# Spreading the shared expert of a mixture-of-experts layer over seven routed experts

## The chip, the cores and the metric

The kernel runs on one core of one Trainium2 chip. The metric is the device time of the whole launch in microseconds. The kernel before took 1259.23 us (median of three runs, 1257.9 to 1260.51). The profile shows one execution of its own, which took 1258.86 us and whose traced span is 1257.0 us.

Engine names in the rows: PE is the matrix engine (TensorE), PEld its weight loads, DVE the vector engine, ACT the scalar engine, POOL GpSimd, SP the sync engine, which here does nothing but wait on semaphores and issue DMAs.

## The reference, cut to what matters

A Perceiver layer on 256 tokens of width 512: cross-attention to 25088 context rows, self-attention with 16 heads, and a mixture of experts. The change is in the last part alone:

```python
shared_out = silu(x @ shared_gate_w) * (x @ shared_up_w) @ shared_down_w    # 512 -> 1024 -> 512
logits = x @ gate_w
topk_ids = argmax(logits); topk_val = max(logits)                           # one of 32 experts for a token
xs = x * sigmoid(topk_val)[:, None]
g = ragged_dot(sorted xs, routed_gate_w)                                    # 32 x 512 x 1024
u = ragged_dot(sorted xs, routed_up_w)                                      # 32 x 512 x 1024
d = ragged_dot(silu(g) * u, routed_down_w)                                  # 32 x 1024 x 512
out = x + shared_out + routed_out                                           # all in float32
```

Every expert has three matrices of 2 MB (2048 KB) each, a gate, an up and a down part. The 32 routed experts are 96 such loads, and all of them are read whatever the routing is.

## The kernel before, in words

The cross-attention fills the span up to about 635 us, then come its last projections, the self-attention (to about 765 us), the router, and from 784.97 us on the experts.

Each engine runs a program of its own, written in the order in which it runs; semaphores tie them together. Nothing is scheduled: what stands later in an engine's program starts later.

**Places for weights.** SBUF holds three sets of places, numbered 0 to 2, each with a place for a gate (`wg`), an up (`wu`) and a down matrix (`wd`), 2 MB each, and one more place for a single gate matrix, `wg_early`, which lies where the token tables of later experts go. Place 0 first holds the shared expert; places 1 and 2 first hold experts 0 and 1; `wg_early` holds the gate of expert 2. These ten loads are issued before the first expert runs (L344 to L366). Every later load goes into a place that some expert has finished with, so SP waits for `gate_done`, `up_done` or `down_done` of that expert, or for `sh_gate_in_psum`, `sh_up_in_psum` or `sh_down_done` of the shared one (L382 to L409). SP's program is one line: a load whose place is free still stands behind an earlier load that waits. All loads go through one queue.

**A routed expert** (`expert`, L794) has up to 32 tokens (a slot tile). PE multiplies gate (L802) and up (L808), ACT makes silu (L1022), DVE the product `hh` (L1347), PE transposes it (L821), ACT copies it out as `hh_t` (L1026), PE multiplies down (L832), DVE copies the result out as `dd` (L1358), and PE scatters it to the tokens into PSUM banks 4 and 5 (L842).

**The shared expert** works on all 256 tokens and is cut into 16 chunks of its gate (0 to 7) and up part (8 to 15), `shared_chunk` (L752), and 8 pieces of its down part (L857). Chunks 0 and 1 run before expert 0. Experts 0 to 3 take three chunks each, put where PE would otherwise wait: behind the up matmuls, behind the transposes, and behind the down matmuls. Then follow, with no routed expert between them, chunks 14 and 15, the eight pieces of the down part in one run, and the token tables of experts 8 to 31.

**Token tables.** `tokens_to_slots` (L778) multiplies the tokens with a selection matrix for eight experts at a time and ACT copies the result out (`slots_out`, L1009). Part 0 is made ahead of expert 0, parts 1 to 3 in one run ahead of expert 4.

**The ring.** From expert 4 on, expert e uses place (e - 4) mod 3, and SP loads expert e + 3 as expert e finishes each of its matrices.

The end: the last expert has matmuls on an identity matrix (`keep_warm`, L462) in its waits, then DVE adds the result to `x` (L1398), which SP stores (L424).

Of the kernel before, what the change touches and what calls it, by code (L numbers as in the profile page):

```python
# [30 lines left out]
E = 32  # L31
FI = 1024
IC = FI // P
GE = 8
SLOT = 32
OV = NQ // SLOT - 1
RING = 3
JG = P // SLOT
# [6 lines left out]
assert NB * BLK == NK and NB % 2 == 1 and (E - 2) % RING == 0 and NSEL == HC * P  # L45
# [21 lines left out]
def perceiver_layer(nc, a):  # L67
    with ExitStack() as ctx:
# [156 lines left out]
        gw_loaded0 gw_loaded1 gw_loaded2 uw_loaded0 uw_loaded1 uw_loaded2 dw_loaded0 dw_loaded1 dw_loaded2  # L225
# [46 lines left out]
        places = [1, 2, 0]  # L272
# [24 lines left out]
        def _(sp):  # L297
# [68 lines left out]
            sp.dma_start(flat(wg_early), g2).then_inc(gw_loaded[1], 16)  # L366
# [12 lines left out]
            g4, u4, d4 = expert_weights(4)  # L379
            g5, u5, d5 = expert_weights(5)  # L380
            g6, u6, d6 = expert_weights(6)
# [3 lines left out]
            sp.wait_ge(s["up_done"], 1)  # L385
            sp.dma_start(flat(wu[1]), u2).then_inc(uw_loaded[1], 16)
            sp.wait_ge(s["down_done"], 1)
            sp.dma_start(down_flat(wd[1]), d2).then_inc(dw_loaded[1], 16)
            next_expert(3, 2, done=2)
            sp.wait_ge(s["sh_gate_in_psum"], IC)  # L390
            sp.dma_start(flat(wg[0]), g4).then_inc(gw_loaded[0], 16)
            sp.wait_ge(s["up_done"], 3)
            sp.dma_start(flat(wu[1]), u5).then_inc(uw_loaded[1], 16)
            sp.wait_ge(s["down_done"], 3)
            sp.dma_start(down_flat(wd[1]), d5).then_inc(dw_loaded[1], 16)
            sp.wait_ge(s["gate_done"], 4)
            sp.dma_start(flat(wg[2]), g6).then_inc(gw_loaded[2], 16)
            sp.wait_ge(s["sh_up_in_psum"], IC)
            sp.dma_start(flat(wu[0]), u4).then_inc(uw_loaded[0], 16)
            sp.wait_ge(s["up_done"], 4)  # L400
            sp.dma_start(flat(wu[2]), u6).then_inc(uw_loaded[2], 16)
            sp.wait_ge(s["sh_down_done"], 1)
            sp.dma_start(down_flat(wd[0]), d4).then_inc(dw_loaded[0], 16)
            sp.wait_ge(s["down_done"], 4)
            sp.dma_start(down_flat(wd[2]), d6).then_inc(dw_loaded[2], 16)
            next_expert(7, 0, done=5)
            with sp.Fori(2, (E - 2) // RING) as g:
                for k in range(RING):
                    next_expert(g * RING + 2 + k, places[k], done=g * RING + k)  # L409
# [46 lines left out]
        def _(pe):  # L456
# [337 lines left out]
            def expert(n, k, rnd, first=False, last_one=False, gate_w=None, shared=()):  # L794

                gate_w = wg[k] if gate_w is None else gate_w
                pe.wait_ge(s["xg_ready"], n + 1)
                pe.wait_ge(gw_loaded[k], rnd)
# [18 lines left out]
                if shared:  # L817
                    shared_chunk(shared[0])
# [4 lines left out]
                if shared:  # L823
                    shared_chunk(shared[1])
# [10 lines left out]
                if shared:  # L835
                    shared_chunk(shared[2])
# [8 lines left out]

            expert(0, 1, 16, first=True, shared=(2, 3, 4))
            expert(1, 2, 16, shared=(5, 6, 7))
            expert(2, 1, 32, gate_w=wg_early, shared=(8, 9, 10))
            expert(3, 2, 32, shared=(11, 12, 13))
            shared_chunk(14)  # L850
            shared_chunk(15)
            pe.wait_ge(s["sh_h_ready"], IC)

            pe.wait_ge(dw_loaded[0], 16)
            for i in range(IC):
                for t in range(QT):
                    last = mm(ps[:, 4 + t, :], h_t[:, i, t * P:(t + 1) * P], wd[0][:, i, :], start=False, stop=True,  # L857
                              skip_group_check=True)
            last.then_inc(s["sh_down_done"], 1)

            for part in range(1, E // GE):
                tokens_to_slots(part)
            expert(4, 0, 32)
            with pe.Fori(1, (E - 2) // RING - 1) as g:
                for k in range(RING):
                    expert(g * RING + 2 + k, places[k], g * 16 + 32)
            for k in range(RING):
                expert(E - RING + k, places[k], 16 * ((E - 2) // RING + 1), last_one=(k == RING - 1))
            pe.wait_ge(s["overflow_known"], 1)
            more = pe.value_load(eo_i[0:1, 7:8], min_val=0, max_val=OV)  # L870
            with pe.If(more > 0):
                tokens_to_slots(E // GE)
                with pe.Fori(0, OV) as o:
                    expert(o + E, 0, o * 16 + 16 * ((E - 2) // RING + 2))
# [3 lines left out]
        def _(act):  # L878
# [141 lines left out]
            def expert(n, more=True, shared=()):  # L1020
                act.wait_ge(s["gate_done"], n + 1)
                act.activation(sg[:, :], ps[:, 0, 0:GW], ACT.Silu).then_inc(s["silu_ready"], 1)  # L1022
                if shared:
                    shared_silu(shared[0])
# [5 lines left out]
                for i in shared[1:]:  # L1030
                    shared_silu(i)
# [5 lines left out]
            expert(0, shared=(2, 3, 4))  # L1037
            expert(1, shared=(5, 6, 7))
            expert(2)
            expert(3)  # L1040
            for part in range(1, E // GE):
                slots_out(part)
            expert(4)
            with act.Fori(1, (E - 2) // RING - 1) as g:
                for k in range(RING):
                    expert(g * RING + 2 + k)
# [13 lines left out]
        def _(dve):  # L1060
# [283 lines left out]
            def expert(n, first=False, shared=()):  # L1344
# [10 lines left out]
                for i in shared[:2]:  # L1355
                    shared_h(i)
                dve.wait_ge(s["down_done"], n + 1)
                dve.tensor_copy(dd[:, :], ps[:, 3, :]).then_inc(s["d_ready"], 1)  # L1358
                for i in shared[2:]:
                    shared_h(i)  # L1360

            expert(0, first=True)
            expert(1)
            for part in range(1, E // GE):
                selection(part)
            expert(2, shared=(0, 1, 2))
            expert(3, shared=(3, 4, 5))
            shared_h(6)
            shared_h(7)
# [17 lines left out]
            expert(4)  # L1387
            with dve.Fori(1, (E - 2) // RING) as g:
                for k in range(RING):
                    expert(g * RING + 2 + k)  # L1390
# [44 lines left out]
```

## Time and profile before

| what | value |
|---|---|
| median of three runs | 1259.23 us |
| the profiled execution | 1258.86 us |
| its span | 1257.0 us |
| first routed expert starts | 784.97 us |
| PE busy over the span | 1117.1 us (89%) |
| DVE, ACT busy | 578.9 us (46%), 392.4 us (31%) |
| DMA, mean over the span | 263 GB/s |
| DMA from 918 to 1242 us | 422 GB/s |

The 40 slices of the page are 31.4 us each. The PE row and the DMA row say which stage an instant belongs to: up to slice 24 PE has the nines and the DMA about half, from slice 28 on the DMA row has nothing but nines and PE falls to 5 to 7 tenths. Slices 24 to 27 lie between, and the change works there. The page's chain that ended last gives 17% of the span to the one line L372 on SP, which is a DMA issue.

### The profile page before, as it was taken

The page shows a single profiled execution, that of the slowest core. Times are in us where ns is not written, and L with a number is a line of the kernel's source. Part 1 is how long each engine was busy: PE and PEld are TensorE (multiplying, and loading weights), DVE is VectorE, ACT ScalarE, POOL GpSimd, SP SyncE. Part 2 cuts the span into 40 slices and gives each one's busy share as a digit, 9 for nine tenths or more (in the row PEclk, how much of TensorE's full clock was granted, in tenths as well). Part 3 has the DMA queues.
Part 4 walks back from the last instruction along what each step waited for, and adds up shares of the span by engine and source line. Part 5 has one row for each costly group of instructions (what it writes and reads, how often), then busy time and mean ns, then how long its engine had stood idle before and what let it go on. Part 6 is the DMA issues. An engine that isn't in the chain of part 4 may idle for free.

```text
span 1257.0 us, 17677 instructions
## 1 busy us (share of the span) xinstructions
PE 1117.1 (89%) x7048; PEld 785.6 (62%) x7048; DVE 578.9 (46%) x955; ACT 392.4 (31%) x645; POOL 3.5 (0%) x20
## 2 busy tenths in 40 slices
PE   9999999999999999999999989998876656665767
PEld 8768888888888888888887657655322222222223
DVE  2367777777777777777743165220110010001001
ACT  1254554554554554554522163101100000000000
POOL 1000000000000000000000000000000000000000
PEclk9999999999999999999999989999998998989988
DMA  9158455455455455455508315997999999999996
GB/s 361 69 224 331 153 194 188 154 192 190 153 191 191 151 191 192 151 190 193 174 1 351 118 67 202 373 380 290 422 418 421 421 425 421 422 422 421 423 419 283
DMA packets 84780, 331.07 MB, mean 263 GB/s; under 512 B 3600, under 2 KB 3728, under 8 KB 75408
## 3 DMA queue, kind: packets, MB, share of 16 engines
q1 hardware_dynamic: 84752, 330.66, 67.7%
q8 instruction: 22, 0.36, 0.1%
q14 instruction: 6, 0.05, 0.0%
HBM read 330.12 MB, written 0.52 MB: 263 GB/s over the span
## 4 chain that ended last, share of the span: by engine, by line
PE 71%; SPq 23%; DMA 3%; DVE 2%; issue 1%; ACT 1%; DVEq 0%
SPq L372 17%; PE ps L507 7%; PE ps L508 7%; PE ps L528 7%; PE ps L509 7%; PE ps L530 7%; PE ps L529 7%; SPq L374 4%; PE ps L516 3%; DMA wu<-in_r_up 2%; SPq L376 2%; PE ps L764 2%; PE ps L482 2%; PE ps L495 2%; PE ps L832 2%; PE ps L802 1%
## 5 line engine op out<-in xcount | busy, mean ns | idle before, releaser
L507 PE MATMUL ps<-ctt_hi,q_hi 128*128 128x512 f32 x392 | 156.9, 400 | 0.9 <-DVE gate L1182 0.9
L508 PE MATMUL ps<-ctt_lo,q_hi 128*128 128x512 f32 x392 | 152.8, 390 | 0.0
L509 PE MATMUL ps<-ctt_hi,q_lo 128*128 128x512 f32 x392 | 152.7, 390 | 0.0
L530 PE MATMUL ps<-nat_hi,pt_lo 128*128 128x512 f32 x392 | 152.7, 389 | 0.0
L528 PE MATMUL ps<-nat_hi,pt_hi 128*128 128x512 f32 x392 | 152.6, 389 | 0.1
L529 PE MATMUL ps<-nat_lo,pt_hi 128*128 128x512 f32 x392 | 152.5, 389 | 0.0
L1347 DVE TENSOR_TENSOR hh<-sg,ps 128x256 f32<-128x256 f32 x32 | 13.5, 421 | 263.0 <-PE ps L808 263.0
L1092 DVE TENSOR_TENSOR nat_lo<-nat,nat_hi 128x2048 fp32r<-128x2048 f32 x49 | 112.3, 2292 | 24.5 <-ACT nat_hi L892 24.5
L832 PE MATMUL ps<-wd,hh_t 128*32 128x512 f32 x512 | 76.9, 727 | 42.3 <-DMA wd<-in_r_down 39.5
L1087 DVE TENSOR_TENSOR ctt_lo<-ctt,ctt_hi 128x2048 fp32r<-128x2048 f32 x49 | 111.9, 2284 | 0.0
L902 ACT ACTIVATE pexp<-ps,st 128x512 f32<-128x512 f32 x98 | 66.6, 686 | 138.6 <-DVE st L1108 138.6
L808 PE MATMUL ps<-wu,xg 128*32 128x256 f32 x1024 | 65.8, 401 | 41.8 <-DMA wu<-in_r_up 41.8
L1114 DVE SCALAR_TENSOR_TENSOR acc<-acc,st,ps 128x512 f32<-128x512 f32 x98 | 68.9, 744 | 70.3 <-PE ps L530 70.3
L896 ACT ACTIVATE pt_hi<-ps 128x1024 fp32r<-128x1024 f32 x49 | 50.3, 1027 | 138.9 <-PE ps L516 138.9
L892 ACT ACTIVATE nat_hi<-nat 128x2048 fp32r<-128x2048 f32 x49 | 93.5, 1908 | 0.0
L888 ACT ACTIVATE ctt_hi<-ctt 128x2048 fp32r<-128x2048 f32 x49 | 93.2, 1902 | 0.0
L1022 ACT ACTIVATE sg<-ps 128x256 f32<-128x256 f32 x32 | 12.3, 384 | 249.6 <-PE ps L802 249.6
L842 PE MATMUL ps<-dd,scat 128*128 128x512 f32 x128 | 70.1, 674 | 21.7 <-DVE dd L1358 21.7
L1358 DVE COPY dd<-ps 128x512 f32<-128x512 f32 x32 | 22.1, 692 | 136.8 <-PE ps L832 136.8
L528 PEld LDWEIGHTS ps<-nat_hi,pt_hi 128*128 128x128 f32 x392 | 73.6, 188 | 15.5 <-issue 0.2
L509 PEld LDWEIGHTS ps<-ctt_hi,q_lo 128*128 128x128 f32 x392 | 73.6, 188 | 15.4
L530 PEld LDWEIGHTS ps<-nat_hi,pt_lo 128*128 128x128 f32 x392 | 73.6, 188 | 15.3
(252 smaller groups left out, 1367.7 us busy)
## 6 DMA issues: line engine op xcount, KB each, us to landing
wu<-in_r_up SPq DMA_DIRECT2D x32, 2048.0 KB, 30.3
wd<-in_r_down SPq DMA_DIRECT2D x32, 2048.0 KB, 34.0
wg<-in_r_gate SPq DMA_DIRECT2D x31, 2048.0 KB, 36.4
ctt<-in_ctx_t SPq DMA_DIRECT2D x49, 1024.0 KB, 5.1
nat<-in_ctx_rows SPq DMA_DIRECT2D x49, 1024.0 KB, 7.4
w_gate<-in_w_g_t SPq DMA_DIRECT2D x2, 1024.0 KB, 11.5
w_k<-in_w_k SPq DMA_DIRECT2D x1, 2048.0 KB, 13.5
w_v<-in_w_v SPq DMA_DIRECT2D x1, 2048.0 KB, 11.7
```

What stands on the lines that cost most here:

```text
L372: sp.dma_start(flat(wg[k]), g).then_inc(gw_loaded[k], 16)
L507: mm(o, qh, ctt_hi[par][:, c, :], start=(c == 0), stop=False)
L508: mm(o, qh, ctt_lo[par][:, c, :], start=False, stop=False)
L509: last = mm(o, ql, ctt_hi[par][:, c, :], start=False, stop=(c == HC - 1))
L528: mm(o, pt_hi[:, q, t, :], nat_hi[par][:, t, :], start=(t == 0), stop=False)
L529: mm(o, pt_hi[:, q, t, :], nat_lo[par][:, t, :], start=False, stop=False)
L530: last = mm(o, pt_lo[:, q, t, :], nat_hi[par][:, t, :], start=False, stop=(t == KT - 1))
L832: last = mm(ps[j * SLOT:(j + 1) * SLOT, 3, :], hh_t[:, m, j * SLOT:(j + 1) * SLOT], wd[k][:, 2 * j + m, :], start=(m == 0), stop=(m == 1))
L888: act.activation(ctt_hi[par][:, :, :], ctt[par][:, :, :], ACT.Copy).then_inc(s["ctt_hi_ready"], 1)
L892: act.activation(nat_hi[par][:, :, :], nat[par][:, :, :], ACT.Copy).then_inc(s["nat_hi_ready"], 1)
L1087: dve.tensor_tensor(ctt_lo[par][:, :, :], ctt[par][:, :, :], ctt_hi[par][:, :, :].bitcast(F32), ALU.subtract).then_inc(s["ctt_lo_ready"], 1)
L1092: dve.tensor_tensor(nat_lo[par][:, :, :], nat[par][:, :, :], nat_hi[par][:, :, :].bitcast(F32), ALU.subtract).then_inc(s["nat_lo_ready"], 1)
```

## The change

The shared expert's work is cut into the same pieces, which are dealt out over the first seven routed experts instead of four: experts 0 to 3 as before, expert 4 takes chunks 14 and 15 and the first two pieces of the down part, experts 5 and 6 three pieces of the down part each. The three token tables 1 to 3 are made one at a time, behind experts 5, 6 and 7. Expert 7 has no shared part.

Place 0 is thus held by the shared expert for longer. Experts up to 7 use places 1 and 2 in turn; only the gate of expert 5 uses place 0, which the shared gate has left. The ring of three places begins with expert 8, expert e using place (e - 8) mod 3. SP's list of loads is written anew for it, the gate of expert 2 gets a semaphore of its own (`early_loaded`), and the vector engine's work on overflowing slot tiles moves from behind expert 3 to behind expert 7.

```diff
+NSH = 8
+        gate_place = [1, 2, None, 2, 1, 0, 2, 1]
+        other_place = [1, 2, 1, 2, 1, 2, 1, 2]
+        shared_work = [(("mid", 2), ("mid", 3), ("mid", 4)), (("mid", 5), ("mid", 6), ("mid", 7)),
+                       (("mid", 8), ("mid", 9), ("mid", 10)), (("mid", 11), ("mid", 12), ("mid", 13)),
+                       (("mid", 14), ("mid", 15), ("down", 0), ("down", 1)), (("down", 2), ("down", 3), ("down", 4)),
+                       (("down", 5), ("down", 6), ("down", 7)), ()]
...
-            sp.wait_ge(gw_loaded[1], 32)
-            sp.wait_ge(s["gate_done"], 1)
-            sp.dma_start(flat(wg[1]), g5).then_inc(gw_loaded[1], 16)
...
+            gate_of(4, 1, done=1)
+            up_of(2, 1, done=1)
+            down_of(2, 1, done=1)
+            gate_of(3, 2, done=2)
+            up_of(3, 2, done=2)
+            down_of(3, 2, done=2)
             sp.wait_ge(s["sh_gate_in_psum"], IC)
-            sp.dma_start(flat(wg[0]), g4).then_inc(gw_loaded[0], 16)
...
+            sp.dma_start(flat(wg[0]), expert_weights(5)[0]).then_inc(gw_loaded[0], 16)
+            up_of(4, 1, done=3)
+            down_of(4, 1, done=3)
...
+            def shared_down(i):
+                pe.wait_ge(s["sh_h_ready"], i + 1)
+                pe.wait_ge(dw_loaded[0], 16)
+                for t in range(QT):
+                    last = mm(ps[:, 4 + t, :], h_t[:, i, t * P:(t + 1) * P], wd[0][:, i, :], start=False, stop=True,
+                              skip_group_check=True)
+                if i == IC - 1:
+                    last.then_inc(s["sh_down_done"], 1)
...
-                if shared:
-                    shared_chunk(shared[0])
+                for kind, i in shared[:1]:
+                    shared_part(kind, i)
                 pe.wait_ge(s["h_ready"], n + 1)
...
-            shared_chunk(14)
-            shared_chunk(15)
-            pe.wait_ge(s["sh_h_ready"], IC)
-            pe.wait_ge(dw_loaded[0], 16)
-            for i in range(IC):
...
-            for part in range(1, E // GE):
-                tokens_to_slots(part)
-            expert(4, 0, 32)
-            with pe.Fori(1, (E - 2) // RING - 1) as g:
...
+            for n in range(NSH):
+                g = gate_place[n]
+                expert(n, wg_early if g is None else wg[g], s["early_loaded"] if g is None else gw_loaded[g], gate_round[n],
+                       other_place[n], other_round[n], first=(n == 0), shared=shared_work[n])
+                if n >= NSH - E // GE + 1:
+                    tokens_to_slots(n - (NSH - E // GE))
...
+            with pe.Fori(0, rounds - 1) as i:
+                for k in range(RING):
+                    ring_expert(i * RING + NSH + k, i, k)
```

Scalar and vector engine follow the same deal (`shared_work`), with `slots_out` behind experts 5, 6 and 7, and the first `gather` of the ring behind the last `slots_out`.

SP's program from the load of expert 6's gate on, before. `wg`, `wu`, `wd` are gate, up and down matrices, the digit behind is the place, and in brackets stands what SP waits for.

```order
L397 DMA wg2_152<-in_r_gate 128x4096 [waits gate_done]
L399 DMA wu0_153<-in_r_up 128x4096 [waits sh_up_in_psum]
L401 DMA wu2_155<-in_r_up 128x4096 [waits up_done]
L403 DMA wd0_156<-in_r_down 128x4x1024 [waits sh_down_done]
L405 DMA wd2_158<-in_r_down 128x4x1024 [waits down_done]
L372 DMA wg0_150<-in_r_gate 128x4096 [waits gate_done]
L374 DMA wu0_153<-in_r_up 128x4096 [waits up_done]
L376 DMA wd0_156<-in_r_down 128x4x1024 [waits down_done]
```

The same place in SP's program now, from the gate of expert 6 to the gate of expert 9.

```order
L392 DMA wg2_152<-in_r_gate 128x4096 [waits gate_done]
L396 DMA wu2_155<-in_r_up 128x4096 [waits up_done]
L400 DMA wd2_158<-in_r_down 128x4x1024 [waits down_done]
L392 DMA wg1_151<-in_r_gate 128x4096 [waits gate_done]
L396 DMA wu1_154<-in_r_up 128x4096 [waits up_done]
L400 DMA wd1_157<-in_r_down 128x4x1024 [waits down_done]
L392 DMA wg0_150<-in_r_gate 128x4096 [waits gate_done]
L396 DMA wu2_155<-in_r_up 128x4096 [waits up_done]
L400 DMA wd2_158<-in_r_down 128x4x1024 [waits down_done]
L422 DMA wu0_153<-in_r_up 128x4096 [waits sh_up_in_psum]
L424 DMA wd0_156<-in_r_down 128x4x1024 [waits sh_down_done]
L392 DMA wg1_151<-in_r_gate 128x4096 [waits gate_done]
```

Before, the second and fourth of these loads wait for the shared expert's up and down part. Now nine loads stand between the gate of expert 6 and the one that waits for `sh_down_done`, and only the last of the nine waits for the shared up part; the gate of expert 9 comes behind them all.

PE's program behind expert 3, before: the rest of the shared expert, three token tables, then expert 4 (its gate matmuls are L802).

```order
L764 MATMUL ps<-y_t_83,wu0_153 128x256 [waits sh_h_ready]
L764 MATMUL ps<-y_t_83,wu0_153 128x256 x3
L857 MATMUL ps<-wd0_156,h_t_87 128x512 [waits dw_loaded0,sh_h_ready]
L857 MATMUL ps<-wd0_156,h_t_87 128x512 x15
L785 MATMUL ps<-gsel_84,y_82 128x256 [waits gsel_ready]
L785 MATMUL ps<-gsel_84,y_82 128x256 x7
L802 MATMUL ps<-wg0_150,xg_89 32x256 [waits gw_loaded0,xg_ready,gather_ready]
```

PE's program now, at expert 6 (gate L846 and up L852, then a piece of the shared down part, L828, in each of its three waits) and the one token table behind it (L815).

```order
L852 MATMUL ps<-wu1_154,xg_89 32x256 x15
L828 MATMUL ps<-wd0_156,h_t_87 128x512 [waits dw_loaded0,sh_h_ready]
L828 MATMUL ps<-wd0_156,h_t_87 128x512
L865 MATMUL ps<-ident_49,hh_91 128x128 [waits h_ready]
L865 MATMUL ps<-ident_49,hh_91 128x128
L828 MATMUL ps<-wd0_156,h_t_87 128x512 [waits dw_loaded0,sh_h_ready]
L828 MATMUL ps<-wd0_156,h_t_87 128x512
L876 MATMUL ps<-wd1_157,hh_t_92 32x512 [waits dw_loaded1,ht_ready]
L876 MATMUL ps<-wd1_157,hh_t_92 32x512 x7
L828 MATMUL ps<-wd0_156,h_t_87 128x512 [waits dw_loaded0,sh_h_ready]
L828 MATMUL ps<-wd0_156,h_t_87 128x512
L815 MATMUL ps<-gsel_84,y_82 128x256 [waits gsel_ready]
```

The 16 matmuls that stood in one run are now in pairs between the matmuls of a routed expert, and one token table follows the expert.

## Rows read from the trace of the kernel before

**Rows 1.** Page, 40 slices: PE's granted clock and DMA share, in tenths.
```profile
PEclk9999999999999999999999989999998998989988
DMA  9158455455455455455508315997999999999996
```

**Rows 2.** Stretches by stage: busy time by engine, then clock, DMA share, GB/s.
```profile
core 0: us, PE busy (x) PEld busy (x) DVE busy (x) ACT busy (x) POOL busy (x), PEclk, DMA share, GB/s
784.97:837.16 52.19, 52.19 (x443) 32.66 (x444) 11.77 (x32) 5.95 (x18) 0.00 (x0) 1.00 0.95 388
868.48:918.10 49.62, 40.12 (x434) 17.03 (x438) 6.89 (x15) 4.83 (x15) 0.00 (x0) 1.00 0.95 390
918.10:1242.50 324.40, 210.00 (x1924) 81.32 (x1923) 30.30 (x66) 21.48 (x67) 0.00 (x0) 0.90 1.01 422
```

**Rows 3.** Two stretches around the change, same columns.
```profile
785.00:790.00 5.00, 5.00 (x72) 3.67 (x73) 2.40 (x10) 0.39 (x1) 0.00 (x0) 1.00 0.37 84
835.00:875.00 40.00, 36.98 (x181) 24.16 (x183) 4.30 (x15) 5.57 (x15) 0.00 (x0) 1.00 0.73 284
```

**Rows 4.** SP's DMA issues: start us, time in the issue, line, tile.
```profile
826.10 0.33 SPq L397 DMA_DIRECT2D wg<-in_r_gate  x1
840.65 0.33 SPq L399 DMA_DIRECT2D wu<-in_r_up  x1
855.16 0.38 SPq L403 DMA_DIRECT2D wd<-in_r_down  x1
870.47 0.34 SPq L372 DMA_DIRECT2D wg<-in_r_gate  x1
```

**Rows 5.** Issue to landing: the loads of L397, L399, L403, and L376's last.
```profile
DMA to landing us min/median/max: 15.1/15.1/15.1
...
DMA to landing us min/median/max: 7.8/7.8/7.8
...
DMA to landing us min/median/max: 7.5/7.5/7.5
...
L376 SPq DMA_DIRECT2D wd<-in_r_down x1: 1179/1179/1179, 1213.0 to 1213.0; - x1
...
DMA to landing us min/median/max: 34.5/34.5/34.5
```

**Rows 6.** Chain that ended last, in order: start us, us, what (784 to 890).
```profile
798.20 1.86 PE ps L802 x32
...
837.16 3.47 PE ps L764 x16
...
841.13 14.00 PE ps L857 x32
...
859.32 4.12 PE ps L785 x16
...
863.90 4.12 PE ps L785 x16
...
878.45 1.86 PE ps L802 x32
...
888.36 1.86 PE ps L802 x32
```

**Rows 7.** The same chain, its end.
```profile
1211.78 30.69 DMA wu<-in_r_up
...
1242.51 1.98 PE ps L808 x32
...
1245.56 2.68 PE ps L462 x48
1248.24 1.85 PE ps L832 x16
...
1251.32 1.79 PE ps L842 x4
```

**Rows 8.** Timeline of PE, two rows: start us, us, line, idle before and releaser.
```profile
943.95 3.45 PE L808 MATMUL ps<-wu,xg 128*32 128x256 f32 x32 [2.98 <-DMA wu<-in_r_up]
...
1236.27 3.78 PE L842 MATMUL ps<-dd,scat 128*128 128x512 f32 x4 [0.79 <-DVE dd L1358]
```

More of the change, by code:

```diff
@@ L44 @@
 MASKED = -1.0e30
-assert NB * BLK == NK and NB % 2 == 1 and (E - 2) % RING == 0 and NSEL == HC * P
+assert NB * BLK == NK and NB % 2 == 1 and (E - NSH) % RING == 0 and NSEL == HC * P
 class Chain:
@@ L402, in _ @@
             sp.wait_ge(s["sh_down_done"], 1)
[L403 to L407, printed above, removed]
+            sp.dma_start(down_flat(wd[0]), expert_weights(8)[2]).then_inc(dw_loaded[0], 16)
+            gate_of(9, 1, done=8)
+            up_of(9, 1, done=7)
+            down_of(9, 1, done=7)
@@ L408, in _, with next_expert @@
+            gate_of(10, 2, done=7)
+            up_of(10, 2, done=8)
+            down_of(10, 2, done=8)
+            def next_expert(e, k, done):
+                gate_of(e, k, done)
+                up_of(e, k, done)
+                down_of(e, k, done)
+            with sp.Fori(1, (E - NSH) // RING) as g:
                 for k in range(RING):
-                    next_expert(g * RING + 2 + k, places[k], done=g * RING + k)
+                    next_expert(g * RING + NSH + k, k, done=g * RING + NSH + k - RING + 1)
@@ L822, in expert @@
                 last.then_inc(s["ht_in_psum"], 1)
-                if shared:
-                    shared_chunk(shared[1])
+                for kind, i in shared[1:2]:
+                    shared_part(kind, i)
                 if last_one:
@@ L834, in expert @@
                 last.then_inc(s["down_done"], 1)
-                if shared:
-                    shared_chunk(shared[2])
+                for kind, i in shared[2:]:
+                    shared_part(kind, i)
                 if last_one:
@@ L844, in expert, with ring_expert @@
                 last.then_inc(s["scatter_done"], 1)
[L846 to L849, printed above, removed]
[L850 to L864 removed]
+            for n in range(NSH):
[4 more added lines that the diff above has]
+                    tokens_to_slots(n - (NSH - E // GE))
+            def ring_expert(n, i, k, **kw):
+                expert(n, wg[k], gw_loaded[k], i * 16 + ring_gate[k], k, i * 16 + ring_other[k], **kw)
+            rounds = (E - NSH) // RING
+            with pe.Fori(0, rounds - 1) as i:
                 for k in range(RING):
[L866 removed]
+                    ring_expert(i * RING + NSH + k, i, k)
             for k in range(RING):
[L868 removed]
+                ring_expert(E - RING + k, rounds - 1, k, last_one=(k == RING - 1))
             pe.wait_ge(s["overflow_known"], 1)
@@ L1022, in expert @@
                 act.activation(sg[:, :], ps[:, 0, 0:GW], ACT.Silu).then_inc(s["silu_ready"], 1)
-                if shared:
-                    shared_silu(shared[0])
+                for kind, i in shared[:1]:
+                    if kind == "mid" and i < IC:
+                        shared_silu(i)
                 act.wait_ge(s["ht_in_psum"], n + 1)
@@ L1029, in expert @@
                     gather(n + 1)
-                for i in shared[1:]:
-                    shared_silu(i)
+                for kind, i in shared[1:]:
+                    if kind == "mid" and i < IC:
+                        shared_silu(i)
             for i in range(2):
@@ L1036, in _ @@
             gather(0)
[L1037 to L1044, printed above, removed]
+            for n in range(NSH):
+                expert(n, more=(n < NSH - 1), shared=shared_work[n])
+                if n >= NSH - E // GE + 1:
+                    slots_out(n - (NSH - E // GE))
+            gather(NSH)
+            with act.Fori(0, (E - NSH) // RING - 1) as i:
                 for k in range(RING):
-                    expert(g * RING + 2 + k)
+                    expert(i * RING + NSH + k)
             for n in range(E - RING, E):
```

81 lines of the change are left out of this document (45 added, 36 removed).

## The prediction

> **What bounds the kernel now.** I read the slices first, then the stretches by stage, then SP's issues and the chain. From slice 28 on the DMA row holds only nines [rows 1]. Between 918.10 and 1242.50 us the DMA share is 1.01 at 422 GB/s while PE is busy for 210.00 of 324.40 us [rows 2]: the ring of routed experts is bound by the loads, without a gap. One 2 MB load (2.097 MB) at 422 GB/s takes 4.97 us. So the end of the kernel is the landing of the last load plus a tail, and everything before it counts only where the queue runs empty. The last load, expert 31's down matrix, is issued at 1213.0 and lands 34.5 us later, at 1247.5 [rows 5]; down matmuls follow at 1248.24 [rows 7].
>
> Where does the queue run empty? At 785 to 790 it moves 84 GB/s [rows 3], ahead of the first load that needs a freed place; the change leaves that. In 835 to 875 it moves 284 GB/s, or 11.36 MB in 40 us, which at 422 would take 26.9 us: **13.1 us are lost** [rows 3]. SP's issues name the causes. After L397 at 826.10 the next issue is L399 at 840.65, for chunk 15 of the shared expert; the next hole ends with L403 at 855.16, for the end of its down part; the third with L372 at 870.47, for expert 4's gate, behind three token tables [rows 4]. A load that finds the queue empty lands 7.8 us after its issue (7.5 for a down matrix) [rows 5], 2.8 us more than its transfer.
>
> A check of that view: L397's load lands at 826.10 + 15.1 = 841.2 [rows 4, 5]. Of 96 loads, 7 are issued before the experts start and 10 more up to this one, so 79 follow: 841.2 + 79 x 4.97 + 13.1 = 1246.9, where 1247.5 is measured.
>
> **The change, part by part.**
>
> *PE's work.* No matmul is added or dropped. A routed expert with three shared parts takes (837.16 - 798.20) / 3 = 12.99 us, one without 888.36 - 878.45 = 9.91 us, a token table 863.90 - 859.32 = 4.58 us, a piece of the shared down part 14.00 / 8 = 1.75 us, a chunk 3.47 / 2 = 1.74 us [rows 6]. Pieces of the down part thus fill the same waits as chunks did. Expert 4 has one part more, 14.7 us from 837.16 to 851.9. Experts 5 and 6 with a table each take 17.6 us: to 869.4 and 887.0. Expert 7 and its table end at 901.5. The trace does not show a table behind an expert, or down pieces in these waits; bounds are 3 us earlier (all further stalls hidden) and 3 us later (a 0.8 us joint at each of several places), and I take the sum as it stands, as its rows are the same instructions.
>
> *The loads.* The queue is FIFO here: a load lands 4.97 us after the one ahead, or 7.8 us after its issue if that is later. Up to expert 6's gate nothing changes: its issues hang on experts 0 to 3, which are as before (landing 841.2). Then, issue and landing: expert 5's up when expert 3's up is done, some 827.8, lands 846.2; its down at 833.6, 851.1; expert 7's gate behind expert 4's gate, 839.1, 856.1; expert 6's up and down, 861.1 and 866.0; expert 8's gate at 853.8, 871.0; expert 7's up and down, the latter issued at some 861, land 876.0 and 880.9; expert 8's up, whose place is free since expert 4, 885.9. Expert 8's down waits for the last shared piece in expert 6, about 869.4 + 13.0 - 1.8 = 880.6; 880.6 + 7.5 = 888.1 is earlier than its turn at 890.9: no hole, 2.8 us to spare. Expert 9's gate waits for expert 7's gate matmuls, 887.0 + 1.9 = 888.9, and lands at 896.7 where its turn would be 895.9: a **hole of 0.8 us**. The four loads behind it wait for nothing later than expert 7's up, its down being the last, at some 895, with its turn at 921.5. Expert 11's gate needs expert 8's gate matmuls, about 903.8, and has until 918.7. From there on it is the ring of before.
>
> No expert waits for weights in this stretch: the tightest are expert 5's up (lands 846.2, wanted at 853.8) and expert 6's up (861.1, wanted at 871.3). This is why two places do: PE needs 13 to 17.6 us for an expert while three loads take 14.9.
>
> *The rest.* The first `gather` of the ring now follows the last table on ACT, some 0.4 us for PE before expert 8, beside 15 us of slack. DVE's overflow work moves behind expert 7 and lies beside a scatter of 1.79 us [rows 7] and a table of 4.58 us [rows 6] on PE; if it isn't covered, the same 15 us take it. The dropped wait on the early gate's load is over when SP gets there. Two register values instead of one per ring expert cost nothing while PE waits for DMA. Bounds for all of these: 0 to 2 us, taken as 0.
>
> *The sum.* Lost before 13.1, lost after 0.8: 12.3 us. By landings, 841.2 + 79 x 4.97 + 0.8 = 1234.6 against 1247.5, 12.9 us. I take 12.4, nearer to the first, since the check above left 0.6 us that may stay. The profiled execution took 1258.86 us, so 1246.5; it lies 0.4 us under the median, within the spread of 2.6 us of the three runs.
>
> A load into an empty queue costs 2.8 us beyond its transfer [rows 5]. The Trainium skill ("DMA: Bandwidth & Descriptors", Latency and other measured facts) gives a fixed cost of some 2 us for a DMA. By that figure, as an estimate, the gate of expert 9 would land at 895.9 and the hole be nothing, so the sum 0.8 us better; the trace's 2.8 us decides.
>
> **The rivals.**
>
> *A: the hole only moves.* Expert 9's gate stands behind all the shared work on SP and on PE. Each microsecond that PE is late at expert 7 makes the 0.8 us hole a microsecond longer, and then also the one at expert 8's down. For it: three joints of table and expert, and the shared pieces wait on semaphores one by one. Against it: the joints of before are 0.5 us each and inside my 4.58 [rows 6]. At 3 to 5 us late, 1249.5 to 1251.5; taken as 1250.5.
>
> *B: the end meets the low clock.* In 918 to 1242 PE was granted 0.90 of 2.4 GHz on average [rows 2], that is short stretches at 1.2 GHz, each after a time with waits for loads. There L808 took 3.45 us for 32 matmuls and L842 3.78 us for four, where the tail of before had 1.98 and 1.79 [rows 7, 8]. In the tail nothing hides that: 1.5 us for the up matmuls and 2.0 us for the scatter, up to twice its 10.0 us of PE pieces if all of it were low. Which matmuls are met changes as the end moves. One or two met: 1248 to 1250.5, taken as 1249.5; all: 1256.5. The Trainium skill ("TensorE: Matmul & The Clock Gate", HAM oscillation) says that a loop whose matmuls are shorter than its DMA waits loses the full clock in every turn; by that rule the tail would begin low, some 3.5 us worse than here. The trace agrees in part: the ring has such stretches, but the tail of before had none.
>
> *C: slower than before.* PE loses the full clock in experts 4 to 7. Expert 9's gate waits for it, so the hole grows by all that PE loses beyond the 0.8: at 12.3 us lost the gain is gone, beyond 14.8 the kernel is slower by more than 0.2%. Experts 5 and 6 with their tables at 1.2 GHz, 35 us more at worst, would give 1281. Against it: PE has no gap in this work and 1.00 of the clock in 784.97 to 918.10 [rows 2].
>
> *D: the change doesn't fill the queue*, because the order of loads holds it up elsewhere, for example a later load of expert 10, and half of the loss stays: 1253.
>
> **How the numbers follow.** Forecast 1246.5, with a chance of 0.56 (its own range 1245 to 1248). A 0.13 at 1250.5, B 0.22 at 1249.5, C 0.03 at 1281, D 0.06 at 1253. A measurement of this kernel tells 0.2%, 2.5 us, from no change; the forecast, A, B and D are all faster by more than that, apart from the far end of B. Faster 0.93, the same 0.04, slower 0.03. The range runs from 1244.0 (hole nothing, PE earlier) to 1251.5, which takes in A and most of B.
>
> **What would show it.** In the profile after: the DMA row with nines from slice 25 on; over 840 to 875 about 420 GB/s; one hole of about a microsecond near 890; SP's longest wait in the stretch at the load for `sh_down_done` or the gate of expert 9; experts 4, 5, 6 starting about 837.2, 851.9, 869.4 and expert 8 at 901.5 to 902; the last landing at 1234 to 1235. A landing later than 1237 says A or D, and the GB/s of 880 to 925 which; a right landing with a tail over 12 us says B. The mechanism is wrong if the stretch is full and the last landing isn't earlier, that is, if the rate of 422 GB/s is not held.

## The result and the profile after

| | before | after |
|---|---|---|
| median, four runs each | 1258.57 us | 1245.78 us (1244.01 to 1245.9) |
| ratio to before, 95% interval | | 0.9893 (0.9876 to 0.991) |
| profiled execution's span | 1257.0 us | 1243.8 us |
| first routed expert starts | 784.97 us | 783.87 us |
| last load lands (issue + time to landing) | 1247.5 us | 1234.4 us |
| from the first expert's start to the last landing | 462.6 us | 450.5 us |
| from there to the end of the span | 9.5 us | 9.4 us |

The forecast was 1246.5 us. The kernel is 12.8 us faster by the medians. The two spans differ by 13.2 us, but 1.1 us of that lies ahead of the first expert, in code that is the same in both (in the profiles of the twelve kernels of this document the first expert starts between 783.1 and 785.9 us): the change moved 12.0 us, and 12.4 were forecast.

The last load, its issue and its time to land:

```profile
1200.09 1.18 SPq L400 DMA_DIRECT2D wd<-in_r_down  x1
DMA to landing us min/median/max: 34.3/34.3/34.3
```

The page's DMA row of the changed kernel, in tenths, and what the 40 slices moved:

```profile
DMA  9258454554554554544606513899999999999996
GB/s 353 81 200 340 169 202 156 181 198 148 193 187 152 200 176 162 202 161 176 205 32 253 221 68 151 338 420 422 401 420 424 423 422 422 422 422 422 422 420 281
```

Counted from 0, the nines run unbroken from slice 26; in [rows 1] from slice 28, behind a seven. Slice 25 has an eight, for the hole at 785 us that the change leaves; the prediction had expected the nines from there on. The stretches that answer to [rows 2, 3], and the two in which expert 9's gate is loaded (start and end, length, busy time by engine, PE's clock, DMA share, GB/s):

```profile
785.00:790.00 5.00, 5.00 (x62) 3.89 (x55) 1.49 (x5) 0.72 (x3) 0.00 (x0) 1.00 0.65 200
835.00:875.00 40.00, 39.53 (x301) 21.11 (x299) 4.28 (x10) 4.44 (x13) 0.00 (x0) 1.00 1.01 419
885.00:890.00 5.00, 4.16 (x66) 2.29 (x66) 0.69 (x2) 0.52 (x3) 0.00 (x0) 1.00 0.93 328
890.00:925.00 35.00, 28.09 (x278) 14.27 (x282) 6.48 (x19) 5.00 (x15) 0.00 (x0) 1.00 1.01 424
918.10:1230.00 311.90, 202.84 (x1854) 77.93 (x1856) 28.92 (x63) 20.68 (x64) 0.00 (x0) 0.90 1.01 422
```

835 to 875 us moves 419 GB/s where it moved 284: 13.1 us were lost there, now 0.3. One small hole is left at 885 to 890: 328 of 422 GB/s over 5 us, 1.1 us. The ring's own rate is the same 422. The row of 785 to 790 is not to be compared with the 84 GB/s of [rows 3]: this kernel's first expert starts 1.1 us earlier, so its first load does too.

SP's issues over the stretch (start us, time in the issue, line, tile), against [rows 4]; seven of them, which are expert 6's gate, 5's up, 7's gate, 8's gate, 8's up, 8's down and 9's gate:

```profile
825.00 0.33 SPq L392 DMA_DIRECT2D wg<-in_r_gate  x1
826.72 0.33 SPq L396 DMA_DIRECT2D wu<-in_r_up  x1
837.99 0.33 SPq L392 DMA_DIRECT2D wg<-in_r_gate  x1
852.67 0.33 SPq L392 DMA_DIRECT2D wg<-in_r_gate  x1
860.54 0.51 SPq L422 DMA_DIRECT2D wu<-in_r_up  x1
879.19 0.38 SPq L424 DMA_DIRECT2D wd<-in_r_down  x1
887.05 0.33 SPq L392 DMA_DIRECT2D wg<-in_r_gate  x1
```

There are still two long pauses between issues, 18.6 and 7.9 us. But when the first begins five loads stand in the queue (the last of them, L422's, lands 24.3 us after its issue), so it doesn't run dry. The load of L424 landed 10.7 us after its issue, which says that it found others ahead of it; an isolated load takes 7.5 to 7.8 us [rows 5]. Expert 9's gate took 7.7. The load ahead of it was still under way when it was issued (L424's landed at 889.89, 2.8 us later), and it landed 4.86 us behind that one, which is its turn (a load's turn: the landing that it has when it follows the load ahead without a hole, 4.97 us behind). The hole shows three landings later, at expert 10's gate:

```profile
888.38 0.81 SPq L392 DMA_DIRECT2D wg<-in_r_gate  x1
```

It lands 22.6 us after its issue, at 910.98, 6.18 us behind the load ahead of it. A landing that comes about 1 us late, one to three loads behind a hole, stands in the other traces too: L374's load in the kernel before comes 6.03 us behind L372's, with which the third hole had ended.

The chain at the joint of experts 4, 5 and 6 (start us, us, what), where pieces of the shared down part (L828) stand in a routed expert's waits:

```profile
845.40 3.63 PE ps L828 x8
849.03 1.72 PE ps L886 x4
850.75 1.86 PE ps L846 x32
852.61 1.73 PE ps L852 x32
854.34 1.91 PE ps L828 x4
856.25 0.23 PE ps L865 x2
856.48 1.72 PE ps L828 x4
858.20 1.85 PE ps L876 x16
860.05 1.91 PE ps L828 x4
861.97 1.72 PE ps L886 x4
```

From 845.40 to 863.68 PE has no gap. Expert 5 takes 850.75 to 863.68 = 12.93 us (12.99 forecast), the table behind it 4.2, and expert 6 starts at 867.87 and expert 7 at 885.06, expert 8 at 899.65. With the 1.1 us of the earlier start added, that is 869.0, 886.2 and 900.8, against 869.4, 887.0 and 901.5.

### The profile page after: what moved, and what is told of

Its sections match the earlier page's. It is cut to its first block, busy times and chain, and to the rows that moved or that the text cites. A ratio compares the mean times of both kernels' runs of the same rounds, so it can differ in the third digit from the quotient of the medians.

```text
span 1243.8 us, 17657 instructions
## 1 busy us (share of the span) xinstructions
PE 1112.1 (89%) x7048; PEld 783.3 (63%) x7048; DVE 579.0 (47%) x955; ACT 392.5 (32%) x645; POOL 3.5 (0%) x20
## 4 chain that ended last, share of the span: by engine, by line
PE 73%; SPq 16%; DMA 8%; DVE 2%; ACT 1%; issue 1%; DVEq 0%
SPq L392 11%; PE ps L537 7%; PE ps L538 7%; PE ps L558 7%; PE ps L539 7%; PE ps L560 7%; PE ps L559 7%; DMA wu<-in_r_up 5%; PE ps L546 3%; SPq L396 3%; DMA wd<-in_r_down 3%; PE ps L794 2%; PE ps L852 2%; PE ps L876 2%; PE ps L886 2%; PE ps L846 2%
## 5 line engine op out<-in xcount | busy, mean ns | idle before, releaser
L852 PE MATMUL ps<-wu,xg 128*32 128x256 f32 x1024 | 64.7, 395 | 38.8 <-DMA wu<-in_r_up 38.8
L1060 ACT ACTIVATE sg<-ps 128x256 f32<-128x256 f32 x32 | 12.3, 384 | 246.0 <-PE ps L846 246.0
```

## The experiments

One number is the clearest for all of them, the time from the first expert's start to the landing of the last load, since it leaves out the stages ahead and the tail. It comes from one profiled execution of each kernel. The last 60 loads, which are the same ring in all twelve, take 298.3 to 298.7 us in ten of them, 299.1 in e5_late6 and 299.5 in e6_tables7, where one landing came 1.1 us late: differences of a few tenths say nothing, and these two carry up to about 1 us that isn't of their edit. The last column is the expectation's difference, by the theory of places (theory 1: the queue runs dry because a load's place is not yet free), put on the kernel that the experiment started from. The first four kernels behind "before" are edits of it, the others are edits of the changed kernel:

| kernel | median us | ratio to before (95%) | to the last landing, us | the same by theory 1 |
|---|---|---|---|---|
| before | 1258.57 | | 462.6 | |
| e1_order | 1258.66 | 1.0002 (0.9991 to 1.0013) | 462.6 | 462.6 |
| e2_tables | 1251.76 | 0.9951 (0.9934 to 0.9968) | 457.1 | 457.0 |
| e3_both | 1251.05 | 0.9944 (0.9928 to 0.9959) | 456.5 | 452.0 |
| e9_warm | 1248.06 | 0.9914 (0.99 to 0.9927) | 452.8 | 451.5 to 452.0 |
| after | 1245.78 | 0.9893 (0.9876 to 0.991) | 450.5 | |
| e6_tables7 | 1247.5 | 0.9907 (0.9878 to 0.9937) | 449.9 | 450.5 |
| e7_tables5 | 1251.69 | 0.9944 (0.9927 to 0.9961) | 456.5 | 456.8 |
| e8_downrun | 1252.37 | 0.9945 (0.9928 to 0.9961) | 455.8 | 456.2 |
| e5_late6 | 1252.1 | 0.9943 (0.9926 to 0.996) | 456.9 | 456.6 |
| e4_late20 | 1267.22 | 1.0073 (1.0057 to 1.0089) | 470.8 | 469.7 |
| e10_parts | 1246.36 | 0.9906 (0.9891 to 0.9921) | 450.9 | 449.3 |

**e1_order**, the kernel before with SP's line alone changed:

```diff
+            sp.wait_ge(s["up_done"], 4)
+            sp.dma_start(flat(wu[2]), u6).then_inc(uw_loaded[2], 16)
+            sp.wait_ge(s["down_done"], 4)
+            sp.dma_start(down_flat(wd[2]), d6).then_inc(dw_loaded[2], 16)
             sp.wait_ge(s["sh_up_in_psum"], IC)
             sp.dma_start(flat(wu[0]), u4).then_inc(uw_loaded[0], 16)
-            sp.wait_ge(s["up_done"], 4)
-            sp.dma_start(flat(wu[2]), u6).then_inc(uw_loaded[2], 16)
             sp.wait_ge(s["sh_down_done"], 1)
             sp.dma_start(down_flat(wd[0]), d4).then_inc(dw_loaded[0], 16)
-            sp.wait_ge(s["down_done"], 4)
-            sp.dma_start(down_flat(wd[2]), d6).then_inc(dw_loaded[2], 16)
```

> The kernel before with two pairs of loads exchanged in SP's line: expert 6's up and down, whose places are free at some 828 and 834 us, go ahead of expert 4's up (free at 841) and down (free at 855). Theory 1, places: the queue runs dry because no place is free, and the last of the holes, the load that waits for expert 4's gate matmuls at 870.5, sets how late all later loads are; filling earlier holes only makes that one larger. 1258.6, the same within 1.5 us, with the loss in one hole of some 10 us ahead of the landing at 878. Theory 2, order on SP: loads stood ready behind loads that waited; then the two holes at 841 and 855 are won, 6.6 us, 1252. Theory 3, work on PE: only stalls of PE that are hidden count; 1258.6.

Measured: no change. Two stretches of it, the columns as above, and SP's issue of the load that waits for expert 4's gate matmuls:

```profile
835.00:855.00 20.00, 19.48 (x57) 11.08 (x56) 3.20 (x12) 0.38 (x1) 0.00 (x0) 1.00 0.88 362
855.00:877.00 22.00, 18.68 (x135) 13.04 (x138) 1.38 (x3) 5.19 (x14) 0.00 (x0) 1.00 0.57 222
```
```profile
868.68 0.33 SPq L372 DMA_DIRECT2D wg<-in_r_gate  x1
```

The early holes are down to 2.8 us (362 of 422 GB/s over 20 us), and the last one has taken the rest: 222 of 422 GB/s over 22 us are 10.4 us, ahead of the load issued at 868.68. Theory 2 is out, which had 6.6 us; theory 3 is not, and e2 decides on it. The holes of before don't add up as three causes. Here only the load with the least slack counts, and that was the load that waited for expert 4's gate, behind the tables.

**e2_tables**, the kernel before with the tables one at a time:

```diff
-            for part in range(1, E // GE):
-                tokens_to_slots(part)
             expert(4, 0, 32)
-            with pe.Fori(1, (E - 2) // RING - 1) as g:
+            tokens_to_slots(1)
+            for k in range(RING):
+                expert(5 + k, places[k], 48)
+                if k < 2:
+                    tokens_to_slots(2 + k)
+            with pe.Fori(2, (E - 2) // RING - 1) as g:
```

and `slots_out` in the same way on ACT.

> The kernel before with the token tables 1 to 3 made one at a time behind experts 4, 5 and 6, in place of all three ahead of expert 4; nothing else. Expert 4 starts 13.7 us earlier (855 in place of 868.5) and its gate's place comes free at 857. Theory 1, places: the hole of 5.6 us at the landing at 878 goes, the two at 841 and 855 stay: 1253.0. Theory 2, order on SP: no change, 1258.6. Theory 3, hidden stalls: PE hides no stall more than before (expert 4 even waits some 3 us for its down matrix), 1258.6.

Measured: 5.4 us off the last landing. 835 to 875 us moves 338 GB/s where it moved 284, so the tables' place is worth 5.4 of the 12.0 us by itself, with no stall hidden; theories 2 and 3 had nothing. Expert 4 now waits for its down matrix, and PE's clock falls behind the wait:

```profile
862.13 3.64 PE L832 MATMUL ps<-wd,hh_t 128*32 128x512 f32 x16 [4.15 <-DMA wd<-in_r_down]
```

The granted clock is 0.57 over 860 to 872 us, the scatter takes 3.78 us, expert 5 starts at 875.07, and still no landing behind it comes late: the two early holes have put off the turns of the loads that wait for expert 5.

**e3_both**, the two edits together:

> The kernel before with both edits, SP's two pairs exchanged and the tables one at a time; the shared down part stays in one run ahead of expert 4, and the ring of three places begins at expert 4 as before. Theory 1, places: only a hole of 2.5 us stays, ahead of expert 4's down matrix (its place is free at 855): 1248.0, so 10.6 us faster, though the first edit alone brings nothing and the second 5.6. Theory 2: as the first alone, 1252. Theory 3: the spreading of the shared down part is what gained, so near 1258.

Measured: 6.1 us instead of 10.6. Theories 2 and 3 had 6.6 and none: the number agrees with theory 2's, but e1 has ruled that one out, and the trace shows another cause. Its timeline of PE, start us, us, line, and in brackets the idle time before and who ended it:

```profile
858.03 0.51 PE L821 MATMUL ps<-ident,hh 128*128 128x128 f32 x2 [0.61 <-DVE hh L1353]
862.84 3.64 PE L832 MATMUL ps<-wd,hh_t 128*32 128x512 f32 x16 [4.30 <-DMA wd<-in_r_down]
867.29 3.78 PE L842 MATMUL ps<-dd,scat 128*128 128x512 f32 x4 [0.81 <-DVE dd L1364]
870.86 4.24 PE L785 MATMUL ps<-gsel,y 128*128 128x256 f32 x16
875.58 1.93 PE L802 MATMUL ps<-wg,xg 128*32 128x256 f32 x32 [0.47 <-ACT xg_all L1016]
```
```profile
860.00:872.00 12.00, 8.35 (x24) 3.17 (x25) 0.69 (x1) 0.00 (x0) 0.00 (x0) 0.57 1.01 426
875.00:880.00 5.00, 3.91 (x66) 2.13 (x66) 0.62 (x2) 0.77 (x2) 0.00 (x0) 1.00 0.43 112
```

Expert 4's down matrix had landed at 862.7, and PE had stood idle for 4.30 us. Behind that wait the granted clock is 0.57 of 2.4 GHz over 12 us, so most of it is at the lower level, 1.2 GHz. The down matmuls take 3.64 us and the scatter 3.78, where 1.92 and 1.98 are usual; expert 5's gate matmuls start at 875.58. The load that waits for them is issued at 877.7 into an empty queue, and 875 to 880 moves 112 GB/s. The expected sum had the wait and not what it does to the clock. In e2 the wait and the low clock were the same and cost the queue nothing; here the early holes are filled, the loads behind have their turns earlier, and the same delay makes two new holes.

**e9_warm** is e3_both with 72 matmuls on an identity matrix in that wait:

```diff
-            expert(4, 0, 32)
+            expert(4, 0, 32, warm=72)
...
+                if warm:
+                    keep_warm(warm, 6)
                 pe.wait_ge(s["ht_ready"], n + 1)
```

> The kernel before with both edits of e3 (SP's two pairs exchanged, tables one at a time), and 72 matmuls on an identity matrix, some 4.0 us, in expert 4's wait for its down matrix. In e3 PE was idle there for 4.3 us, was then granted 1.2 GHz at about 862 to 871, and the work behind (down matmuls 3.64 us in place of 1.92, scatter 3.78 in place of 1.98) came late enough for two new holes, 2.9 and 0.8 us. Theory, the low clock made these holes: down and scatter take 1.9 and 2.0 us again, the holes go, and the kernel takes 1247.5 to 1248, about what e3 was to take. Rival, the down matrix itself is late and what follows is late with it whatever the clock: 1251, as e3.

Measured: 3.7 us off e3's last landing, most of the 4.5 us it had missed. The same place:

```profile
858.21 4.18 PE L462 MATMUL ps<-identb 128*128 128x128 bf16 x72
862.47 1.93 PE L834 MATMUL ps<-wd,hh_t 128*32 128x512 f32 x16
865.20 1.98 PE L844 MATMUL ps<-dd,scat 128*128 128x512 f32 x4 [0.81 <-DVE dd L1366]
867.02 3.88 PE L785 MATMUL ps<-gsel,y 128*128 128x256 f32 x16
871.37 1.93 PE L802 MATMUL ps<-wg,xg 128*32 128x256 f32 x32 [0.47 <-ACT xg_all L1018]
```
```profile
860.00:872.00 12.00, 10.65 (x91) 7.70 (x92) 0.69 (x1) 1.53 (x4) 0.00 (x0) 1.00 1.01 425
875.00:905.00 30.00, 24.17 (x214) 14.92 (x214) 3.44 (x8) 5.50 (x16) 0.00 (x0) 1.00 1.01 416
```

The clock is full where e3 had 0.57, expert 5 starts 4.2 us earlier, and the queue stays full to 905. So the low clock made e3's new holes: nothing but useless work was added. Its other expectation, 1251 us, did not come. And with the shared down part still in one run and the three-place ring still starting at expert 4, the kernel before comes to within 2.3 us of the change by the last landing (by whole times it isn't told apart from it: the intervals of the two ratios overlap a little).

**e4_late20** and **e5_late6** put 360 and 108 such matmuls ahead of expert 7 of the changed kernel:

```diff
+                if n == 7:
+                    keep_warm(360, 6)
```

> The changed kernel with 360 matmuls on an identity matrix (some 20 us of PE) ahead of expert 7. Its gate's place is what the load of expert 9's gate waits for. Theory 1, places: that load has no slack left (its landing is at its turn), so nearly all of the 20 us come back as a hole: 1265, slower than the kernel before. The rival, that this stretch has slack and the rest is bound by the rate alone: PE is ahead of the loads by 15 us at expert 8, so only some 5 us of 20 come back, 1251.

> The changed kernel with 108 matmuls on an identity matrix (some 6 us) ahead of expert 7: the second point of the curve whose first was 360 of them and 21.4 us. Places: no slack is left at expert 9's gate, so all 6.1 us come back, 1251.9. If the stretch had a microsecond or two of slack that 20 us only hid: 1250.

Measured: 20.3 and 6.3 us on the last landing for 20.3 and 6.1 us of PE. e4's PE row, its issue of expert 9's gate, and the stretch:

```profile
885.88 20.27 PE L492 MATMUL ps<-identb 128*128 128x128 bf16 x360 [0.47 <-ACT xg_all L1053]
```
```profile
880.01 0.38 SPq L424 DMA_DIRECT2D wd<-in_r_down  x1
908.08 0.33 SPq L392 DMA_DIRECT2D wg<-in_r_gate  x1
```
```profile
885.00:915.00 30.00, 27.62 (x446) 23.41 (x446) 2.25 (x7) 1.15 (x3) 0.00 (x0) 1.00 0.33 124
```

A late expert 7 comes back nearly one for one, though PE is then some 15 us ahead of the loads at expert 8. By the landing of expert 10's gate, ahead of the ring's scatter, it is 5.6 us for 6.1 and 20.2 for 20.3, so a slack of half a microsecond isn't excluded. It is not PE's lead over the weights that is short but the queue's lead over the places. With 20 us the changed kernel is slower than the one before: rival C's way from a late expert 7 to a slower kernel is real, and by this slope the gain is gone at some 12 us. Its cause, a low clock in this stretch, did not occur.

**e6_tables7** and **e7_tables5** put all three tables behind expert 7, or behind expert 5:

```diff
-                if n >= NSH - E // GE + 1:
-                    tokens_to_slots(n - (NSH - E // GE))
+                if n == 7:
+                    for part in range(1, E // GE):
+                        tokens_to_slots(part)
```

and `slots_out` on ACT in the same way; e7 has `n == 5`.

> The changed kernel with the three token tables in one run behind expert 7. Expert 7 then starts 9.2 us earlier and expert 8 when it did. Places: expert 9's gate has its turn already without a hole, so nothing is won or lost, 1245.8 within 1 us. The rival, that tables one at a time are of use in themselves: slower by some us, as expert 8 waits for them all.

> The changed kernel with the three token tables in one run behind expert 5. Expert 6, in which the last piece of the shared down part lies, starts 9.2 us later, expert 7 4.6 us later. Expert 8's down matrix then is issued at some 888.4 in place of 879.2, where its turn allows 882.1: a hole of 6.3 us, and expert 9's gate finds its turn behind it without one: 1252.1. If instead the worst single delay at expert 9's gate counted, 4.6 us: 1250.4. If tables cost nothing wherever they stand: 1245.8.

Measured: behind expert 7 the last landing comes 0.6 us earlier; its median of 1247.5 us is not told apart from 1245.8 (the intervals of the ratios overlap). Behind expert 5 it comes 6.0 us later. The issue that paid, and its stretch, in e7:

```profile
861.72 0.51 SPq L422 DMA_DIRECT2D wu<-in_r_up  x1
889.53 0.38 SPq L424 DMA_DIRECT2D wd<-in_r_down  x1
```
```profile
885.00:895.00 10.00, 9.80 (x90) 3.83 (x88) 0.75 (x2) 0.38 (x1) 0.00 (x0) 1.00 0.43 158
```

The same 13.7 us of PE work cost nothing behind expert 7 and 6.0 us behind expert 5. One at a time is not better than all at once, if all at once stands behind the last matmuls that free a place that the queue is short of. In e6 the stretch of the small hole, 885 to 890, moves 427 GB/s where the changed kernel has 328: its 1.1 us are gone. Only 0.6 us are seen in the last landing, since e6's ring took 1.2 us longer than the changed kernel's; by the landing of expert 10's gate it was 1.7 us ahead.

**e8_downrun** puts the eight pieces of the shared down part in one run behind expert 4:

```diff
-                       (("mid", 14), ("mid", 15), ("down", 0), ("down", 1)), (("down", 2), ("down", 3), ("down", 4)),
-                       (("down", 5), ("down", 6), ("down", 7)), ()]
+                       (("mid", 14), ("mid", 15)), (),
+                       (), ()]
...
+                if n == 4:
+                    for i in range(IC):
+                        shared_down(i)
```

> The changed kernel with the eight pieces of the shared down part in one run behind expert 4, so that experts 5 and 6 have their waits bare; chunks 14 and 15 stay in expert 4, tables, places and loads as changed. Expert 5 starts some 11 us later, expert 7 some 6 us later. Places: a hole of 1.7 us at expert 8's gate and one of 4.0 us at expert 9's gate, 1251.5. The rival, that only the order of loads and tables counts: 1245.8.

Measured: 5.3 us later. Expert 5 starts at 863.49 and expert 7 at 891.81; with 1.6 us taken off, by which this run's first expert started later, that is 11.1 and 5.1 us behind the changed kernel. Two places are then short: expert 8's gate waits for expert 5's, expert 9's for expert 7's. The expectation had the total (5.7 us) but not its parts: 1.7 and 4.0 us were expected, and the two gates land 3.1 and 2.3 us behind their turns, with 1.0 us more three landings later. So within the changed order of loads the spreading of the down part is worth 5.3 us: it fills some 5 us of stalls in experts 4 to 6, and it doesn't stand as 14 us ahead of expert 5.

**e10_parts** went for what is left: expert 4's gate in four loads, each behind a quarter of expert 0's gate matmuls, and fewer matmuls on the identity matrix at the end.

```diff
+            for c in range(HC):
+                if c < HC - 1:
+                    sp.wait_ge(s["gate_part"], c + 1)
+                else:
+                    sp.wait_ge(s["gate_done"], 1)
+                sp.dma_start(flat(wg[1])[:, c * FI:(c + 1) * FI], expert_weights(4)[0][:, c * FI:(c + 1) * FI]
+                             ).then_inc(s["g4_loaded"], 16)
...
-                    keep_warm(48, 6)
+                    keep_warm(36, 6)
...
-                    keep_warm(20, 6)
+                    keep_warm(12, 6)
```

> The changed kernel, aimed at what is left of it: the first load into a freed place (expert 4's gate) is cut into four, each issued as a quarter of expert 0's gate matmuls is done, which brings its first byte some 1.4 us forward; and the matmuls that keep the clock up in the last expert are cut from 48 and 20 to 36 and 12, since the last load lands 0.65 us before the 48 end. Places: the hole of 6 us at 785 shrinks by 1.2 us and the tail by 1.1 us, 1243.5. Rivals: the quarters cost more at their ends than they win, 1245; or the tail is met by 1.2 GHz with fewer such matmuls, 1246 to 1248.

Measured: nothing won, 1246.36 us. The next load behind the four landed at 799.0 us, as in the changed kernel (799.1), and 0.3 us later when counted from the first expert's start, so what the quarters won at their beginning they lost by their end. And the tail met the low clock, as rival B had it (granted clock 0.50 over 1230.4 to 1232.4 us); its rows, with the changed kernel's own row of the up matmuls below:

```profile
1229.36 3.05 PE L860 MATMUL ps<-wu,xg 128*32 128x256 f32 x32 [2.23 <-DMA wu<-in_r_up]
1233.47 2.17 PE L498 MATMUL ps<-identb 128*128 128x128 bf16 x36
1235.58 1.92 PE L884 MATMUL ps<-wd,hh_t 128*32 128x512 f32 x16
```
```profile
1229.39 1.93 PE L852 MATMUL ps<-wu,xg 128*32 128x256 f32 x32 [1.89 <-DMA wu<-in_r_up]
```

The up matmuls stand ahead of the matmuls that were cut, so the cut didn't cause it. It cost 1.1 us, what the shorter runs would have won.

## Why the prediction was right

*The bound.* "The landing of the last load plus a tail" held: the tail of the changed kernel is 9.4 us against 9.5, those of the experiments 9.2 to 10.8, and each kernel's median moved as its last landing did, to within 1.7 us.

*The three holes as 13.1 us.* Right in size by the stretch's GB/s. But the prediction named three causes as if each had its price, and e1 shows that they had one: the first two could be filled for nothing in return.

*The sum.* 12.4 us forecast and 12.0 measured agree better than their parts do. The prediction let nothing change up to the landing of expert 6's gate; from the first expert's start that landing came 0.8 us earlier (55.4 us after it, before 56.2). SP issues the first load into a freed place 2.0 us after that start in the profiles of the changed kernel and of those made from it with that load in one piece, and 2.4 us after it in all with the old list; by that landing they have 55.4 to 55.8 and 55.9 to 56.4 us. Why isn't known: the dropped wait was over by then (`wg_early` had landed at 784.7). Behind that landing the change won 11.2 us, not 12.3: beside 79 loads of 4.97 us each the kernel before lost 13.7 us and the changed one 2.5, where 13.1 and 0.8 were reckoned. That the two differences have opposite signs is luck. The sum by landings, 12.9 us, was 0.9 too high.

*PE's sum.* Expert 5 12.93 us (12.99), starts of experts 6, 7 and 8 within 0.8 us. The joints that the trace of before did not show cost nothing; the table at 4.2 us was a little cheaper than 4.58.

*The loads.* Expert 8's down matrix was issued with its turn still ahead (10.7 us to land), and expert 9's gate was the one at the edge. The hole, 0.8 us forecast, is 1.1 us by the GB/s of its stretch. This too is part luck. With the 1.1 us of the earlier start added the gate was issued at 888.15, 0.75 us earlier than forecast, and by the prediction's rule (7.8 us after the issue, or the turn if that is later) the hole would have been 0.1 us. The rule leaves out the 1.2 us that come only at expert 10's gate.

*The rivals.* A and D did not happen; e4 and e5 show that A's slope of one for one is right or nearly so, and e7, whose hole stands at another load, comes to 1251.7 us where D had 1253 for one of its kind. B did not happen in the profiled tail, but it did in those of e8, e9 and e10: their up matmuls of the last expert take 3.25, 3.27 and 3.05 us in place of 1.93, and the tails are up to 1.4 us longer. The 3.5 us that the prediction set beside B, for a tail that begins low, had as their condition a loop whose matmuls are shorter than its waits; in this ring PE is busy for 210.00 of 324.40 us [rows 2], so they had no ground. C did not happen, but e4 shows what a late expert 7 costs.

*What the prediction had wrong in its argument.* It took the spread of the shared expert, the tables and the new places as one thing. Alone, the tables' place gives 5.4 us (e2); with SP's exchange and a kept-up clock, 9.8 us (e9) come without spreading the down part at all.

Not settled: the 2.3 us between e9 and the change. e9 has a hole of 2.9 us ahead of expert 4's down matrix, which is place 0's and free only after the shared down part, and the changed kernel has its own of 1.1; the remaining 0.5 us isn't placed. That was reckoned from the landings, and no run removed it.

## What to carry to other kernels

Where a stream of loads bounds a kernel and loads go into places that work must free, write down for each load its turn to land and the time at which its place comes free plus the time that an isolated load takes to land (7.5 to 7.8 us here). The largest excess of the second over the first is what is lost, give or take 1 us here, and filling a hole ahead of that load alone wins nothing (e1). Work that frees no place belongs behind the work that frees one, and a stall in front of a freeing matmul can cost twice, once for itself and once for the lower clock behind it: in e3, where the queue was short of that place, and not in e2, where it was not.

## What the runs showed of the hardware

The wait in e3 of 4.3 us on PE took the granted clock to 0.57 over the 12 us from 860 on and made 3.9 us of matmuls (1.92 + 1.98) into 7.4; 72 small bf16 matmuls in the wait kept it at 1.00 (e9). The same kind of wait costs nothing in the ring (2.98 us ahead of L808 [rows 8], clock 0.90 and 422 GB/s [rows 2]), where it is followed by another wait for the loads.

A load into an empty queue was not the constant that the prediction used. Expert 4's gate landed 8.3 us after its issue in the changed kernel, and the same load 7.8 to 8.4 us after it in the experiments made from that kernel with the load in one piece, where [rows 5] have 7.5 and 7.8 and L424 in e7 has 7.3. Expert 4's down matrix in e3 took 8.9, but the load ahead of it landed 1.1 us after its issue. What makes the difference wasn't found.

Behind a hole the whole loss is not in the first landing: 6.18 us between two landings in the changed kernel, 6.03 in the one before, 6.28 in e4 and 6.37 in e7, where 4.8 to 5.2 us are usual in the ring.

In the ring SP is held in the issue itself. With at most five loads that had not landed an issue took 0.3 to 0.8 us, but for one of 3.6; with six or more, 0.3 to 13.8 us (kernel before and changed kernel).

Four loads of a quarter in place of one gave no earlier end, with 0.5 MB each and SP's issues spread over 784.2 to 786.6 us.
